# The per-sample mixing of a two-layer FFN kernel as 64-row by 64-column products, in two PSUM banks

## What is computed

```python
# layer 0, per sample b (cut)
att = softmax(gelu(gelu(cond @ W0 + b0) @ W1 + b1) @ W2 + b2)      # [B, 8]
agg_w = einsum('bk,koi->boi', att, weight)                          # [B, 32, 32]
y = einsum('boi,bih->boh', agg_w, x) + (att @ bias_k)[:, :, None]   # the mixing
x = x + y @ W_up.T + lora_delta(y, argmax(y @ gate_w.T + expert_bias))
# layer 1
c = grouped_conv1d(x, 9 taps, 4 groups) + ctx + fside
x = x + c @ W_base.T + b_base + lora_delta(c, top-2 of softmax(c @ W_gate.T))
```

## Time and profile before

| | before |
|---|---|
| runs | 374.01, 376.78, 377.02 us; median 376.78 |
| profiled execution | 375.63 us, its span 373.8 us |
| mean granted clock of TensorE | 0.981 of full speed |
| TensorE products, weight loads | 94% and 92% of the span |
| VectorE, GpSimd, ScalarE | 64%, 54%, 36% |

### The profile page before, as it was taken

How to read it: one execution, slowest core, us unless ns; L and a number is a source line. 1 busy time by engine, 2 the same in 40 slices (tenths; PEclk the granted TensorE clock), 3 DMA queues, 4 the chain that set the end, 5 groups by cost and what they waited for, 6 DMA issues and landing times.

```text
span 373.8 us, 9133 instructions
## 1 busy us (share of the span) xinstructions
PE 352.3 (94%) x2593; PEld 345.5 (92%) x2593; DVE 237.9 (64%) x977; ACT 135.5 (36%) x410; POOL 200.1 (54%) x229
## 2 busy tenths in 40 slices
PE   2879999699999999999999999999999999999985
PEld 1667999699999999999999999999999999999974
DVE  1675868366666666667667666666667667666653
ACT  2634344133344343333333343333343433343330
POOL 8467555505566655455555566555545545656430
PEclk9996899899999999999999999999999999999999
DMA  7633278513333333333233333343323333332221
GB/s 158 184 103 57 95 181 180 114 26 76 75 78 85 85 85 85 83 65 77 54 80 76 74 82 85 85 85 85 84 57 61 77 79 74 76 84 57 59 57 58
DMA packets 54302, 31.98 MB, mean 86 GB/s; under 512 B 43869, under 2 KB 44301, under 8 KB 54289
## 3 DMA queue, kind: packets, MB, share of 16 engines
q1 hardware_dynamic: 40064, 27.69, 30.1%
q10 hardware_dynamic: 13984, 3.73, 7.1%
q0 software_dynamic: 240, 0.41, 0.5%
HBM read 14.35 MB, written 8.93 MB: 62 GB/s over the span
## 4 chain that ended last, share of the span: by engine, by line
PE 84%; DVE 3%; DMA 3%; issue 1%; SPq 1%; POOL 1%; ACT 1%; ACTq 0%; DVEq 0%
PE ps_base L1080 18%; PE ps_up L919 17%; PE ps_base L1085 9%; PE ps_up L924 8%; PE ps_mix L983 7%; PE ps_mix L941 6%; PE ps_conv L941 6%; PE ps_base L1057 6%; PE ps_up L966 3%; DMA xq<-x1s 2%; PE ps_turn L950 1%; PE ps_turn L958 1%; DMA mix_all<-agg_mix 1%; SPq L294 1%; POOL base_p L425 1%
## 5 line engine op out<-in xcount | busy, mean ns | idle before, releaser
L475 POOL TENSOR_TENSOR y_lo<-y,y_hi 128x512 fp32r<-128x512 f32 x31 | 40.0, 1290 | 127.5 <-ACT y_hi L529 127.5
L1080 PE MATMUL ps_base<-base_hi,c_hi 128*128 128x392 f32 (+1 forms) x256 | 78.2, 322 | 1.8 <-ACT c_hi L575 1.3
L1080 PE MATMUL ps_base<-base_lo,c_hi 128*128 128x392 f32 (+1 forms) x256 | 75.3, 311 | 0.0
L919 PE MATMUL ps_up<-up_hi,y_hi 128*128 128x292 f32 (+1 forms) x256 | 72.3, 305 | 3.1 <-DMA mix_all<-agg_mix 3.1
L919 PE MATMUL ps_up<-up_lo,y_hi 128*128 128x292 f32 (+1 forms) x256 | 70.0, 294 | 0.0
L454 POOL TENSOR_TENSOR xq_lo<-xq,xq_hi 128x260 fp32r<-128x260 f32 x64 | 47.6, 744 | 26.9 <-ACT xq_hi L511 26.9
L463 POOL TENSOR_TENSOR x1b<-x1s,bbase_s 128x256 f32<-128x256 f32 x64 | 56.6, 911 | 0.0
L919 PEld LDWEIGHTS ps_up<-up_hi,y_hi 128*128 128x128 f32 x256 | 49.2, 192 | 4.1 <-issue 4.1
L1080 PEld LDWEIGHTS ps_base<-base_hi,c_hi 128*128 128x128 f32 x256 | 48.2, 188 | 2.3 <-DVE ot L762 2.2
L919 PEld LDWEIGHTS ps_up<-up_lo,y_hi 128*128 128x128 f32 x256 | 49.2, 192 | 0.0
L1085 PE MATMUL ps_base<-base_hi,c_lo 128*128 128x392 f32 (+1 forms) x256 | 48.4, 311 | 0.0
(11 more groups left out here) (178 smaller groups left out, 661.6 us busy)
## 6 DMA issues: line engine op xcount, KB each, us to landing
xt<-in_x SPq DMA_DIRECT2D x32, 256.0 KB, 2.6
out_x<-ot SPq DMA_DIRECT2D x32, 256.0 KB, 2.0
xq<-x1s SPq DMA_DIRECT2D x160, 32.5 KB, 2.1
xq<-x1s ACTq DMA_DIRECT2D x96, 32.5 KB, 2.2
rows<-agg_rows SPq DMA_DIRECT2D x2, 597.0 KB, 4.7
wbase_raw<-in_L_ffn_W_base SPq DMA_DIRECT2D x2, 512.0 KB, 4.2
rows<-agg_rows SPq DMA_DIRECT2D x1, 598.0 KB, 4.4
wup_raw<-in_L_ffn_W_up ACTq DMA_DIRECT2D x2, 256.0 KB, 4.5
```

Of the source, the lines that this page charges most:

```text
L475: pool.tensor_tensor(y_lo[:], y32[:], y_hi[:], ALU.subtract).then_inc(ylo_done, 1)
L919: pe.matmul(into, y_hi[:, k], w[:, k, cols], start=(k == 0 and w is up_hi), stop=False, skip_group_check=True)
L1080: pe.matmul(ps_base[:, j, 0:width], c_hi[:, q], w[:, q, j, 0:width], start=(q == 0 and w is base_hi), stop=False, skip_group_check=True)
```

## The change

Tiles 0 and 1 (WHOLE = 2) keep the products of 128x128. From tile 2 on, each chunk of `xt` is multiplied in two halves of the partitions, rows 0 to 63 and rows 64 to 127, each with the 64 columns of its own two samples: 8 products of 64 rows by 64 moving columns, in place of 4. The stationary operand of each is 64 rows by 128 columns of `xt`. The first half writes to the first bank of `ps_pair`, the second to the second; these are the former `ps_mix` and `ps_conv`, so that the mixing now also waits for ScalarE to have emptied `ps_conv`. `y_sum` reads 256 columns of each bank.

`mix_all` holds only 64 columns per tile, since each half has its blocks in the same columns. TensorE doesn't read it any more: VectorE copies the tile's 128x64 to `mix_s` in two pieces of 32 columns (`mix_pick`), where the two memsets of the layer-1 gate stood. With that the wait for the DMAs of `mix_all` goes from TensorE to VectorE, at the same place of the program.

```diff
+WHOLE = 2
-        ps_mix, ps_conv, ps_turn, ps_ct = (bank(n) for n in ("ps_mix", "ps_conv", "ps_turn", "ps_ct"))
+        ps_pair, ps_turn, ps_ct = bank("ps_pair", 2), bank("ps_turn"), bank("ps_ct")
+        ps_mix, ps_conv = ps_pair[:, 0:1], ps_pair[:, 1:2]
-        mix_all = sb("mix_all", [P, NT, P])
+        mix_all, mix_s = sb("mix_all", [P, NT, P // 2]), sb("mix_s", [P, P // 2])
...
-                        sp.dma_start(mix_all[rows_s, :, rows_s],
+                        sp.dma_start(mix_all[rows_s, :, s % 2 * C:(s % 2 + 1) * C],
...
+            def mix_pick(t, half):
+
+                cols = slice(half * C, (half + 1) * C)
+                dve.tensor_copy(mix_s[:, cols], mix_all[:, bass.ds(t, 1), cols].rearrange("p t o -> p (t o)"))\
+                    .then_inc(mixw_done, 1)
...
-                dve.tensor_tensor(y32[:], ps_mix[:, 0].rearrange("p (k r) -> p k r", k=KC),
...
+                    mixed = ps_pair[:, :, 0:HALF].rearrange("p s (k r) -> p k s r", k=KC)
+                    dve.tensor_tensor(y32[:].rearrange("p k (s r) -> p k s r", s=2), mixed,
+                                      rows[:, bass.ds(t * P, P)].rearrange("p (s r) -> p s r", s=2).unsqueeze(1)
+                                      .to_broadcast([P, KC, 2, P // 2]), ALU.add).then_inc(y32_done, 1)
...
                     if soon(i + 1):
                         mix_blocks(i + 1, 0)
+                    elif once(i + 1):
+                        mix_pick(i + 1, 0)
                     else:
                         dve.memset(beat[:], 0.0)
...
+                if isinstance(i, int) and i == FIRST - 1:
+                    dve.wait_ge(mix_in, 16 * SPT)
...
-                if isinstance(t, int) and t < SOON:
-                    pe.wait_ge(mixw_done, (t + 1) * 2)
-                    weights = mix_w[:].rearrange("p b o -> p (b o)")
-                else:
-                    weights = mix_all[:, bass.ds(t, 1), :].rearrange("p t o -> p (t o)")
+                pe.wait_ge(mixw_done, (t + 1) * 2)
+                weights = mix_w[:].rearrange("p b o -> p (b o)")
...
+                if once(t - 2):
+                    pe.wait_ge(c32_done, (t - 1) * SPT)
                 for k in range(KC):
-                    mm = pe.matmul(ps_mix[:, 0, k * P:(k + 1) * P], xt[:, par, k * P:(k + 1) * P], weights,
-                                   start=True, stop=True)
...
+                        for s in range(2):
+                            half = slice(s * P // 2, (s + 1) * P // 2)
+                            w2 = weights[half, half] if soon(t) else mix_s[half]
+                            mm = pe.matmul(ps_pair[:, s, k * P // 2:(k + 1) * P // 2],
+                                           xt[half, par, k * P:(k + 1) * P], w2, start=True, stop=True)
...
-                if isinstance(i, int) and i == FIRST - 1:
-                    pe.wait_ge(mix_in, 16 * SPT)
```

More of the change, by code:

```diff
@@ L642, in y_sum @@
                 after(dve, ylo_done, t)
-                dve.tensor_tensor(y32[:], ps_mix[:, 0].rearrange("p (k r) -> p k r", k=KC),
-                                  rows[:, bass.ds(t * P, P)].unsqueeze(1).to_broadcast([P, KC, P]),
-                                  ALU.add).then_inc(y32_done, 1)
+                if isinstance(t, int) and t < WHOLE:
+                    mixed = ps_mix[:, 0].rearrange("p (k r) -> p k r", k=KC)
+                    dve.tensor_tensor(y32[:], mixed, rows[:, t * P:(t + 1) * P].unsqueeze(1).to_broadcast([P, KC, P]),
+                                      ALU.add).then_inc(y32_done, 1)
+                else:
+                    mixed = ps_pair[:, :, 0:HALF].rearrange("p s (k r) -> p k s r", k=KC)
+                    dve.tensor_tensor(y32[:].rearrange("p k (s r) -> p k s r", s=2), mixed,
+                                      rows[:, bass.ds(t * P, P)].rearrange("p (s r) -> p s r", s=2).unsqueeze(1)
+                                      .to_broadcast([P, KC, 2, P // 2]), ALU.add).then_inc(y32_done, 1)
             dve.wait_ge(cond_turned, 1)
@@ L782, in body @@
                         mix_blocks(i + 1, 1)
+                    elif once(i + 1):
+                        mix_pick(i + 1, 1)
                     else:
@@ L981, in mix @@
                     pe.wait_ge(c32b_done, t - 1)
+                if once(t - 2):
+                    pe.wait_ge(c32_done, (t - 1) * SPT)
                 for k in range(KC):
-                    mm = pe.matmul(ps_mix[:, 0, k * P:(k + 1) * P], xt[:, par, k * P:(k + 1) * P], weights,
-                                   start=True, stop=True)
+                    if isinstance(t, int) and t < WHOLE:
+                        mm = pe.matmul(ps_mix[:, 0, k * P:(k + 1) * P], xt[:, par, k * P:(k + 1) * P], weights,
+                                       start=True, stop=True)
+                    else:
+                        for s in range(2):
[3 more added lines that the diff above has]
+                                           xt[half, par, k * P:(k + 1) * P], w2, start=True, stop=True)
                 mm.then_inc(mix_done, 1)
```

## The result

| | before | after |
|---|---|---|
| runs | 374.01 to 378.68, median 376.9 us (4) | 382.68 to 382.89, median 382.71 us (4) |
| ratio | | 1.0163, 95% interval 1.0099 to 1.0227 |
| profiled execution, span | 375.63, 373.8 us | 382.68, 380.9 us |
| mean granted clock | 0.981 | 0.991 |
| PE, PEld, DVE | 94%, 92%, 64% | 94%, 91%, 69% |

The change made the kernel slower by 1.6%, 5.8 us by the medians and 7.1 by the two spans. I had forecast 409 us, in a range of 386 to 418.

The account below looks back on a forecast made before the run. TensorE was taken to bound every steady tile. Per tile 1.71 (loads) + 0.33 (switching) - 0.89 (old mixing) = +1.15 us, times 30 = +34.5, less 0.9 for the moved wait: 375.63 + 33.6 = 409 us, range 386 to 418.

Parts of the forecast that it names:

- The loads of the mixing: TensorE's mixing: 16 loads one behind the other at 0.107 us, 1.71 us a tile in place of 0.89.
- The bound below it: Mixing loads: shortest pace of load and product in the trace, 0.064 us from 32-row transposes, hence 1.02 us a tile.
- rival A: Mixing: loads of the two halves run side by side at 0.064 us, +0.46 us a tile, 389 us; chance 0.32.
- the multiplier: Tiles 2 to 31: the per-tile sum of +1.15 us counted for 30 tiles, +34.5 us.
- The change of the row count: TensorE around the mixing: 0.15 us lost going in and 0.18 going out, 0.33 us a tile.
- The control at the lower clock: Two 8-column products (L894) start 0.20 us apart: read as the load at 1.2 GHz, 0.10 at 2.4 GHz.
- The moved wait: Wait for mix_all, from TensorE at end of body 3 to VectorE: gain of 0.9 us (0 to 1.7).
- VectorE: Gate copies of 192 ns each make hw under 0.4 us later, hidden by a cover of 1.6 us.
- The forecast's own range: Whole kernel with serial loads: 400 to 418 us, given chance 0.50.
- B: Mixing: both halves' products run together, loads cost no more than products; -0.13 us a tile, 371 us; chance 0.04.
- C: Mixing: loads paired (8 x 0.107), half the switching cost; +0.14 us a tile, 379 us, no measurable change; chance 0.06.
- D: TensorE pays the change between halves too (448 us), or the clock falls (up to 51 us more); chance 0.08.

Follow-up runs that it names:

- e1: The changed kernel with the mixing's four products of rows 0 to 63 first, then the four of rows 64 to 127: 397.3 us.
- e3: The changed kernel with 32 moving columns per product instead of 64, the second sample of each half left out: 385.33 us.
- e4: The changed kernel with the mixing of tiles 3 to 31 in two visits, around the six products of the second LoRA term: 395.15 us.
- e10: The changed kernel with whole 128x128 products again, only the last of the four chunks multiplied in halves: 382.24 us.
- e6: The changed kernel, with TensorE too waiting for mix_all at the end of body 3, as in the kernel before: 385.75 us.
- e9: The changed kernel with VectorE's two picks per tile as reductions over a one-element axis in place of copies: 385.7 us.

## Why the prediction was wrong

- **What bounds the kernel**: right. TensorE sets every steady tile, before and after, and the period rose by what its own rows lost.
- **The loads of the mixing**: the step that failed. "I take 0.107, because in every row the loads follow one another": every row that I had was of loads into the same rows. Loads into different halves run side by side, and the 16 cost 0.89 us, not 1.71: the term was +0.82 us a tile and is 0. That is 25 us of the 26 by which the forecast missed. That a load's time does not depend on its rows, and that the loads and not the products set the pace, was right (e1, e3).
- **The bound below it** was no bound. The 0.064 us of the 32-row transposes was taken for the least time of a load with its product, but those sixteen all lie in the same 32 rows; with two halves the pace is 0.056. At 0.064 the 16 would cost 0.13 us more, 3.9 us in all. This is why the result is outside the range, whose lower end rested on rival A with that pace. Rival A had the right mechanism: with 0.056 in place of 0.064 its 389 us become 385. What is left to 382.7 is about the multiplier and the hidden wait for `ot`, below.
- **The change of the row count**: right, and in size too: 0.33 us a tile forecast from the first 22 us of the trace, 0.35 measured at the edges of the mixing, shown per visit by e4 and e10. The period rose by 0.30 only, as the longer mixing hides 0.04 us of waiting for `ot`, which the sum did not have.
- **The control at the lower clock** (L894): it rests on the distance of 0.20 us alone. No row of the granted clock shows half there, the stretch from 9.0 to 10.5 us reads 1.00. The sum does not use it.
- **The multiplier**: 30 tiles, where the price of 26 is in the sum of the spans; the other four lie in the start and the end, whose sums hardly moved. 1.2 us less.
- **The moved wait**: -0.9 forecast, -0.8 between mixings 4 and 5 in the trace. The agreement is luck: 0.5 of it is that the DMAs landed earlier after mixing 4, and 0.3 the moved wait; the half clock behind the stand came, as forecast, but did not in e1, e4 and e10. TensorE stood before hw for 1.94 us, not 3.0, because the DMAs had landed at 72.4 and not 73.1 and the gate with its first two picks took 1.7 us and not 1.9.
- **VectorE**: covered, as forecast, but with the copies at 0.54 us and not 0.19 the cover shrank from 1.6 to 0.7 or 0.8 us. A wrong term that by luck cost nothing.
- **The forecast's own range**: its upper end adds up to 417, not 418.
- **Rivals B, C, D**: B came true in part (both halves' products do run together, starting 7 ns apart where the rival's text has 4), but the loads and the switch leave nothing of it. C's loads "paired" at 8 x 0.107 is what happened, with the full cost of switching in place of half. In D neither the change between the halves cost anything (0.007 us between their starts) nor did the clock fall.

## What to carry to other kernels

Splitting a product by rows halves the moving columns of each and lets the two halves run together, loads too; but every half needs the load of the whole width, so where loads set the pace nothing is won, and each visit to the smaller products costs 0.35 us at the full clock. By this arithmetic it could pay only where the moving columns are many beside the loaded ones; no run here shows such a case. And a least pace taken from rows that all use the same part of a resource is no bound for work that uses different parts.

## What the runs showed of the hardware that was not expected

- Loads into rows 0 to 63 and into rows 64 to 127 start 0.007 us apart and run beside each other; two loads with their products take 0.111 us, one takes the same.
- TensorE does not keep the two halves in step: with all of one half ahead in the program, a second series of starts, 0.11 us apart like the first, began when the first had started five of its eight loads.
- Going from 128-row to 64-row products and back costs 0.35 us, for 4 records in halves as for 16 (e10, changed kernel).
- A VectorE copy of 128x32 waits for the end of GpSimd's operation (0.48 to 0.85 us in place of 0.18), a reduction that reads and writes the same does not (0.186).
- Behind a stand of about 2 us the clock was granted in half for 3.4 us in some executions (changed kernel, 1.94 us) and not in others (e10, 2.25 us), worth 1.5 us. Which of the two, no run explains.
- Mixing 4 begins at 65.2, 66.3 and 66.7 us in three kernels that are the same up to there (changed, e6, e9), the part behind the last mixing takes 28.0, 29.1 and 29.4 us, and the period of the steady tiles is 10.52 us in all three.
